# Keys, values and transposes of a full step moved between the score blocks of a second cross-attention layer

## The reference

```python
x = x + _L1_xattn_ref(_layernorm(x, axis=-1), ctx_1024, ctx_1024, wq, bq, wk, bk, wv, bv, wo, bo)

def _L1_xattn_ref(query, key, value, wq, bq, wk, bk, wv, bv, wo, bo):
    NUM_HEAD, DIM_HEAD = 16, 16
    Q = proj(query, wq, bq)        # x @ w.T + b, split into 16 heads of 16
    K = proj(key, wk, bk)
    V = proj(value, wv, bv)
    energy = einsum('bhqd,bhkd->bhqk', Q, K) / sqrt(DIM_HEAD)
    attn = softmax(energy, axis=-1)
    out = einsum('bhqk,bhkd->bhqd', attn, V)
    return out.transpose(0, 2, 1, 3).reshape(B, S, DIM) @ wo.T + bo
```

## Time and profile before

| | |
|---|---|
| median of 3 runs | 1888.92 us (1888.12 to 1889.22) |
| the profiled execution, its own time | 1879.97 us |
| its span | 1878.3 us, mean granted clock of PE 0.93 |
| busy, share of the span | PE 85%, PEld 64%, DVE 60%, ACT 42%, POOL 27% |
| `cross1`, t = 9 to 40 | 1151.6 to 1678.2 us, by the first exponential of each step |

### The profile page before, as it was taken

How to read it: one execution, slowest core, us unless ns; L and a number is a source line. 1 busy time by engine, 2 the same in 40 slices (tenths; PEclk the granted TensorE clock), 3 DMA queues, 4 the chain that set the end, 5 groups by cost and what they waited for, 6 DMA issues and landing times. The chain is left out here.

```text
span 1878.3 us, 26909 instructions
## 1 busy us (share of the span) xinstructions
PE 1603.4 (85%) x10311; PEld 1193.4 (64%) x10311; DVE 1122.9 (60%) x1784; ACT 790.6 (42%) x1084; POOL 500.8 (27%) x630
## 2 busy tenths in 40 slices
PE   5989999999999668779997787998999899875299
PEld 3777777777777457558887564555665555433288
DVE  3976666666652465356665798777666777005641
ACT  3545555555544132224442223555555555651110
POOL 0004434434469000000000202444333544640000
PEclk9999999999999877679999999999999899997599
DMA  2122212212222100022221110110010010000253
GB/s 79 57 57 68 66 48 68 65 49 68 57 57 46 34 1 1 22 92 81 77 95 38 34 46 23 35 35 24 23 35 23 25 33 12 1 1 23 90 170 110
DMA packets 75443, 92.35 MB, mean 49 GB/s; under 512 B 7442, under 2 KB 62276, under 8 KB 75332
## 3 DMA queue, kind: packets, MB, share of 16 engines
q1 hardware_dynamic: 75140, 90.79, 16.3%
q10 hardware_dynamic: 192, 0.05, 0.0%
HBM read 73.47 MB, written 0.52 MB: 39 GB/s over the span
## 5 line engine op out<-in xcount | busy, mean ns | idle before, releaser
L591 POOL CAST st<-ef 32x512 fp32r<-32x512 f32 x384 | 233.5, 608 | 369.2 <-PE score L1173 325.6
L1744 DVE TENSOR_REDUCE mx<-bank 128x1 f32<-128x512 f32 x384 | 246.9, 685 | 96.8 <-PE bank L1188 96.1
L777 ACT ACTIVATE P<-score 128x1024 f32<-128x1024 f32 x256 | 251.3, 1023 | 124.7 <-PE score L1173 124.6
L977 PE MATMUL bank<-c_hi,w_split 128*128 128x512 f32 x640 | 223.6, 407 | 26.1 <-DVE c_lo L1601 16.1
L1173 PE MATMUL score<-qs,st 97*128 97x512 f32 x512 | 174.1, 429 | 16.8 <-ACT P L777 11.5
L1188 PE MATMUL bank<-ef,qm 128*128 128x512 f32 x384 | 151.1, 445 | 30.1 <-DVE mx L1744 21.0
L977 PEld LDWEIGHTS bank<-c_hi,w_split 128*128 128x128 f32 x640 | 122.9, 192 | 73.6 <-issue 22.4
L556 POOL TENSOR_TENSOR sum<-sum,P 128x512 f32<-128x512 f32 x84 | 111.1, 1323 | 209.9 <-ACT P L693 209.9
L693 ACT ACTIVATE P<-score 128x1024 f32<-128x1024 f32 x128 | 130.0, 1025 | 78.5 <-PE score L1011 76.1
L977 PE MATMUL bank<-w_split,c_hi 128*128 128x256 f32 x768 | 145.7, 289 | 5.4 <-ACT v L787 5.4
L1188 PEld LDWEIGHTS bank<-ef,qm 128*128 128x128 f32 x384 | 73.1, 192 | 100.5 <-DVE mx L1744 80.5
(11 more groups left out here) (320 smaller groups left out, 2809.4 us busy)
## 6 DMA issues: line engine op xcount, KB each, us to landing
c_in<-in_ctx SPq DMA_DIRECT2D x64, 512.0 KB, 3.9
w<-k SPq DMA_DIRECT2D x128, 128.0 KB, 2.2
arena<-in_L_ffn_w SPq DMA_DIRECT2D x16, 1024.0 KB, 5.2
arena<-in_L_ffn_W SPq DMA_DIRECT2D x16, 1024.0 KB, 5.5
x<-in_x SPq DMA_DIRECT2D x1, 512.0 KB, 3.7
raw<-in_L_xattn_Wk SPq DMA_DIRECT2D x1, 512.0 KB, 6.5
raw<-in_L_xattn_Wv SPq DMA_DIRECT2D x1, 512.0 KB, 7.3
raw<-in_L_xattn_Wq SPq DMA_DIRECT2D x1, 512.0 KB, 8.2
```

The lines of the kernel that those rows point to most:

```text
L591: pool.tensor_copy(st1[32 * block:32 * block + 32, k, :], ef1[rows, g % LAG, part, :].bitcast(F32)).then_inc(a[f"st{k}"], 16)
L777: act.activation(P1[:, index % PRING, :], score[n % 2][:], ACT.Exp).then_inc(a["p"], 1)
L977: last = mm(dst, l, r, start=(n == 0), stop=(n == len(pairs) - 1))
L1744: v.tensor_reduce(mx1[:, u % 2, i, n:n + 1], bank_of(a, g + 1, f"m{n}")[:], AX.X, ALU.max).then_inc(a["red"], 1)
```

## The change

Three edits, all in `cross1`. The numbers of lines behind the change are up to 15 higher: L964 becomes L972, L977 L985, L1173 L1181, L1188 L1196, L1201 L1210, L1601 L1616, L1744 L1759, L1755 L1770.

1. A full step now transposes the next chunk, t + 1, and does so behind blocks 6 and 7. Keys stand behind block 1 and values behind blocks 3 and 5. The mixture's second half moves behind block 1 of the next step. All eight blocks have their two maxima behind them. In steps with i = 0 (t = 16, 24) keys, mixture, values, shift row and transposes stay behind block 7. From t = 33 on, each block has one mixture block behind it, four blocks late.
2. `order1` follows, and serves all steps.
3. The ring `ef1` of keys gets ten slots (`ERING`) in place of nine; other buffers move to make room.

```diff
+ERING = LAG + 1
-        ef1 = at("ef1", 0, [LAG, 2, CHUNK], F32R)
-        v1 = at("v1", 9216, [VRING, KT, 16, 17])
+        ef1 = at("ef1", 0, [ERING, 2, CHUNK], F32R)
+        v1 = at("v1", 10240, [VRING, KT, 16, 17])
...
-        wout1 = at("wout1", 31104, [4, D])
+        wout1 = at("wout1", 50176, [4, D])
...
-        order1 = ["t0", "t1", *(f"m{n}" for n in range(16)), "k0", "v0", "v1"]
-        early1 = ["k0", "v0", "v1", "t0", "t1"]
+        order1 = [*(f"m{n}" for n in range(16)), "k0", "v0", "v1", "t0", "t1"]
...
             if kind == "m":
-                return ("red", 16 * (t - 1) + n + 1) if t <= CHUNKS else None
-            chunk = t + (kind == "t" and t < LAG)
-            if not 0 <= chunk < CHUNKS or (kind == "t" and t < LAG <= chunk):
+                return ("red", 16 * (t - 1) + n + 1) if LAG <= t <= CHUNKS else None
+            chunk = t + (kind == "t")
+            if not 0 <= chunk < CHUNKS:
                 return None
...
@@ ScalarE, a full step
                     for n in range(8):
                         weights(g, n)
-                        if n in (1, 4) and t < CHUNKS:
-                            context_high(a, c_hi, t, t, n // 4)
...
+                        if i and t < CHUNKS:
+                            if n == 1:
+                                keys(t)
+                            if n in (3, 5) and u % 2 == 0:
+                                values(u, i, n // 2 - 1)
+                            if n >= 6 and t + 1 < CHUNKS:
+                                context_high(a, c_hi, t, t + 1, n - 6)
...
@@ TensorE, a full step
-                    ahead_of = 8 if i == 0 else 7 if u % 2 else 6
                     for n in range(8):
...
                         scores(g, n)
-                        if t <= CHUNKS and n < ahead_of:
+                        if t <= CHUNKS:
                             maxima(t - 1, n)
-                        if n in (1, 4) and t < CHUNKS:
-                            turn(a, t, t, n // 4)
-                        if n == 1 and t > CHUNKS + 1 and g % NCH:
-                            mixture(g - 1, 1)
-                        if n == 5:
-                            mixture(g, 0)
-                    if t < CHUNKS:
-                        keys(t)
-                    if t <= CHUNKS and ahead_of < 8:
-                        maxima(t - 1, ahead_of)
-                    if t <= CHUNKS or g % NCH == NCH - 1:
-                        mixture(g, 1)
-                    if t <= CHUNKS and ahead_of < 7:
-                        maxima(t - 1, 7)
-                    if t < CHUNKS and u % 2 == 0:
-                        values(t, 0)
-                    if i == 0 and t <= CHUNKS:
-                        shift_row(u - 1)
-                    if t < CHUNKS and u % 2 == 0:
-                        values(t, 1)
+                            if n == 1 and g % NCH:
+                                mixture(g - 1, range(4, 8))
+                            if n == 5:
+                                mixture(g, range(4))
+                        elif n >= 4:
+                            mixture(g, (n - 4,))
+                        elif t > CHUNKS + 1:
+                            mixture(g - 1, (n + 4,))
+                        if i and t < CHUNKS:
+                            if n == 1:
+                                keys(t)
+                            if n in (3, 5) and u % 2 == 0:
+                                values(t, n // 2 - 1)
+                            if n >= 6 and t + 1 < CHUNKS:
+                                turn(a, t, t + 1, n - 6)
+                    if i == 0:
+                        if t < CHUNKS:
+                            keys(t)
+                        mixture(g, range(4, 8))
+                        if t < CHUNKS and u % 2 == 0:
+                            values(t, 0)
+                        if t <= CHUNKS:
+                            shift_row(u - 1)
+                        if t < CHUNKS:
+                            if u % 2 == 0:
+                                values(t, 1)
+                            turn(a, t, t + 1, 0)
+                            turn(a, t, t + 1, 1)
...
@@ VectorE, a full step
-                    ahead_of = 8 if i == 0 else 7 if u % 2 else 6
                     for h in range(HPU1):
-                        if LAG <= t < CHUNKS and h == min(ahead_of + 1, 7):
-                            if ahead_of < 8:
-                                low_keys(t)
                         if LAG <= t <= CHUNKS:
                             reduce(t - 1, h)
...
-                        if t < LAG and h == 1:
+                        if (t < LAG and h == 1) or (i and LAG <= t < CHUNKS and h == 2):
                             low_keys(t)
-                        if LAG <= t < CHUNKS and h in (2, 5):
-                            context_low(a, c_hi, c_lo, t, t, h // 4)
                     if i == 0 and 0 < t <= CHUNKS:
                         maximum(u - 1)
-                    if LAG <= t < CHUNKS and ahead_of == 8:
+                    if i == 0 and LAG <= t < CHUNKS:
                         low_keys(t)
                     if g > 0 and g % NCH == 0:
                         finish(g // NCH - 1)
-                    if t + 1 < LAG:
+                    if t + 1 < CHUNKS:
                         for f in range(2):
                             context_low(a, c_hi, c_lo, t, t + 1, f)
```

More of the change, by code:

```diff
@@ L590, in stage_keys @@
                     for block, part in ((0, 0), (1, 0), (2, 1)):
[L591 removed]
+                        pool.tensor_copy(st1[32 * block:32 * block + 32, k, :], ef1[rows, g % ERING, part, :].bitcast(F32)).then_inc(a[f"st{k}"], 16)
                         pool.wait_ge(a[f"st{k}"], a.n(f"st{k}", 48 * g + 16 * block + 16))
@@ L819, in cross1 @@
                             values(u, i, 1)
-                        if t + 1 < LAG:
-                            for f in range(2):
-                                context_high(a, c_hi, t, t + 1, f)
+                        for f in range(2):
+                            context_high(a, c_hi, t, t + 1, f)
                         if t == NCH:
@@ L1187, in maxima, with mixture @@
                         dst = score[h % 2][:, 512 * q:512 * q + 512] if early else place_free(a, g + 1, f"m{2 * h + q}")[:]
-                        mm(dst, qm1[:, h, 128 * q:128 * q + 128], ef1[:, g % LAG, 0, :], start=True, stop=True).then_inc(a["ms"], 1)
-                def mixture(g, quad):
+                        mm(dst, qm1[:, h, 128 * q:128 * q + 128], ef1[:, g % ERING, 0, :], start=True, stop=True).then_inc(a["ms"], 1)
+                def mixture(g, blocks):
                     u, i = divmod(g, NCH)
-                    if i == 0 and quad == 0:
-                        clear_mix(a, u)
-                    if quad == 0:
-                        pe.wait_ge(a["v"], a.n("v", values1(u, i) + 2))
-                    for k in range(KT):
-                        index = 8 * g + 4 * quad + k
+                    for n in blocks:
+                        quad, k = divmod(n, 4)
+                        if n == 0:
+                            if i == 0:
+                                clear_mix(a, u)
+                            pe.wait_ge(a["v"], a.n("v", values1(u, i) + 2))
+                        index = 8 * g + n
                         pe.wait_ge(a["p"], a.n("p", index + 1))
```

41 lines of the change are left out of this document (16 added, 25 removed).

## The result

The changed kernel takes 1961.22 us (median of four runs, 1951.45 to 1965.97), the kernel before 1888.52 us in the same comparison. The ratio is 1.0383, with a 95% interval of 1.0336 to 1.0429: it is slower by 72.7 us. The forecast was 1951, range 1924 to 1978, slower with a chance of 0.93. The way, the place and most of the size were right. In the stage itself the sum had 62 us and the profiled execution shows 73; about half of the 11 us between them are shown to be the clock in ordinary steps (E6).

A forecast was written before the change was run, and what follows sets the result against it. PE and DVE handing two PSUM banks back and forth were taken as the bound. Stretch terms of +18.7, +13.0, +12.2, +8.7, +12.8, +1.6, -5.3 and +0.6 gave +62 us, a median of 1951, range 1924 to 1978.

The forecast's parts named there:

- the sum: Fourth stage, t = 8 to 40: gains and losses of all stretches added, together +62 us.
- The second transpose waits for a `c_lo` behind all reductions: Full steps: PE waits before transpose f=1 for DVE's subtraction of f=0, behind sixteen reductions; 1.7 us a step.
- the lower bound: Steps with transposes: if `c_lo` found a gap before the last two reductions, 1.3 us less loss each; +33 in all.
- An odd-unit step takes 19.0, with low queries 20.1: Steps without values: 19.0 us in place of 16.1; low queries ahead of the reductions add 1.06.
- The split of the loss: Odd-unit step: of +2.9 us, 1.7 is the wait before the second transpose, 1.2 uncovered maxima in blocks 3 to 5.
- PE's own work of 13.3 us: Odd-unit step before the change: matmuls, keys, mixture and transposes sum to 13.3 us of 16.1.
- the circle: Odd-unit step: schedule of PE, ACT and DVE from one `c_lo` of f=0 to the next, closing at 19.0 us.
- Steps t = 16 to 18 and the half clock after `finish`: Unit edge: 25.2, 27.2 and 22.9 us, plus 2.5 for half clock; 77.8 for 64.8.
- The clock stays up in ordinary steps: Full steps away from `finish`: short waits leave the granted clock at 1.00, so the sum adds nothing.
- rival A: Ordinary steps: the clock falls there too, 10 to 32 us more, 1961 to 1983; chance 0.11 beyond the forecast.
- Rival B: Full steps: DVE limits less than scheduled, half the loss hidden; +15 to +45, 1904 to 1934; chance 0.14.
- C: Even-unit steps: values between blocks cover the waits for reductions; faster, median about 1882; chance 0.04.

The follow-up runs named there:

- E6: Changed kernel with 24 matmuls of zeros before the second transpose and 12 before the maxima of block 1: 1953.71 us, ratio 1.0366.
- E1: Changed kernel with `c_lo` of f=0 moved on DVE ahead of the last two reductions: 1949.55 us, ratio 1.0339.
- E10: E1 with matmuls of zeros (24 or 8, none at i = 1) before the maxima of block 1: 1926.61 us, ratio 1.0214.
- E3: Kernel before with only the mixture of t = 33 to 40 placed as in the change: 1878.16 us, ratio 0.997.
- E8: Changed kernel with maxima over half of each bank, so shorter reductions: 1902.55 us, one run.
- E7: Kernel before with maxima over half of each bank, so shorter reductions: 1839.25 us, one run.
- E5: Changed kernel with steps of i = 0 (t = 16, 24) placed like all other full steps: 1963.87 us, ratio 1.043.
- E9: E3 with transposes of its own chunk behind blocks 0 and 2, keys, values and mixture pairs spread, and `c_lo` and `low_keys` moved: 1852.22 us, ratio 0.9832.
- E4: Changed kernel with transposes, keys, values and mixture pairs spread evenly over the blocks: 1864.44 us, ratio 0.989.

## Why the prediction was right, and where it fell short

- *The second transpose waits for a `c_lo` behind all reductions:* right. 43.2 us in 22 waits, 1.4 to 2.2 us in twenty of them (1.7 in the forecast), 6.5 behind `finish` (5.4 + 1.7). E1 moves only that instruction, E10 it with zeros, and both get 1.26 us back in t = 30 at full clock, the 1.3 of the lower bound; E10 has 18.7 less than E6 in t = 9 to 30.
- *An odd-unit step takes 19.0, with low queries 20.1:* 19.03 and 20.2. *An even one 21.8:* 21.77 (t = 23), 22.13 (t = 22).
- *The last seven steps 9.8:* 9.76, shown alone by E3.
- *The split of the loss:* too much for uncovered maxima, too little for the chain (E8). PE's own work of 13.3 us was too small as well (14.5 without any idle time in E7; the sum of 38 matmuls at 0.24 is 9.1, not 8.9), but the circle, which gave the 19.0, doesn't use it.
- *Steps t = 16 to 18 and the half clock after `finish`:* 77.5 for 77.8, and this is luck. By steps 25.2, 27.2 and 25.4 were forecast and 28.1, 25.8 and 23.5 came: the first was 2.9 too short, the others 3.3 too long together. In t = 24 to 26, 2.1 over, it is the same, +3.9, +0.8 and -2.5. The lower clock didn't come behind `finish` alone: the granted clock was 0.94, 0.89, 0.94 in t = 16, 17, 18 and 0.84, 0.77, 0.98 in t = 24, 25, 26.
- *The clock stays up in ordinary steps (rival A apart from it, chance 0.11):* this is the step that failed. It fell in some ordinary steps, at full price in few: t = 20 took 25.05 for 22.93, t = 10 22.03 for 20.41. Filling the waits gives 5.4 us in the ordinary steps of this execution, and 13.0 would have been to gain in E5's. The sum had nothing for it, and A (10 to 32 us, up to 1.7 in 19 steps) began too high: one execution lies between the two cases that I had kept apart, the other inside A. A step with a fallen clock can also lose more than 1.7 (t = 15 took 21.69 in E5 for 19.16). The clock goes with the spread: two runs of the changed kernel with a mean granted clock of 0.911 and 0.912 took 1965.97 and 1964.98 us, two with 0.919 took 1951.45 and 1957.46. In t = 31 to 33 the clock was 0.90, and 2.0 us are missing there, but it was 0.92 before too: what this part owes to the clock is not shown.
- *Rival B (half of the loss hidden) and C (the values' cover wins):* refuted by the step lengths. That covering waits can win is shown by E9, with another order.

Open in part: the 1.7 us that t = 30 keeps over the kernel before in E1 and E10. E1's trace says where they lie: PE is idle 1.0 us for reductions and `c_lo` there against 0.2 before, and six of its eight pairs of maxima take 0.73 to 1.10 us instead of 0.63, before three. That the lump of mixture and keys and the uncovered blocks 3 to 5 are the reason is read from the timeline; no run took the lump alone apart.

## What to carry to other kernels

When a piece is moved to a new place in one engine's order, follow its answer through every other engine's order: here a subtraction of 0.68 us became late only because it stood behind sixteen reductions. Two uses of one bank in a row need the whole round (write, copy, subtract) between them, so put as much other work there. Spread pieces so that each handed-over bank has some work behind it, and check for every kind of step that the work is really there: in E4 two blocks of each odd step had none behind them. And price a new wait twice: once for its length, once for the slower clock it can leave behind, which can also take back the gain when the wait is shortened.

## What the runs showed of the hardware

I had not expected that added matmuls of zeros shorten a stretch: t = 10 to 15 took 122.6 us without and 119.0 with 216 more matmul records, because the granted clock went from 0.93 to 1.00. Nor that a stop of 1.5 us can be enough for the lower clock, and need not be. At the edge to t = 20 the clock fell behind such a stop and before the next one, of 0.7 us: the pair of maxima at 1403.76 already takes 1.05 us, 0.63 at full clock.

```profile
1402.71 0.66 PE L972 MATMUL bank<-ident,c_in 128*128 128x128 f32 x4 [1.51 <-DVE c_lo L1616]
1403.12 0.84 PE L1181 MATMUL score<-qs,st 97*128 97x512 f32 x2
...
1403.76 1.05 PE L1196 MATMUL bank<-ef,qm 128*128 128x512 f32 x2
...
1406.40 1.39 PE L1196 MATMUL bank<-ef,qm 128*128 128x512 f32 x2 [0.73 <-DVE mx L1759]
...
1407.72 3.21 PE L1210 MATMUL bank<-P,v 128*17 128x256 f32 x32
```

The same two waits, 1.48 and 0.60 us, left t = 30 at full speed, and the same instructions kept the clock in t = 27 in the changed kernel's trace and lost it in E5's. The Trainium skill, "TensorE: Matmul & The Clock Gate", section "A second HAM failure mode: psum-queue depth-cycling", tells of such a swing between the two levels from short pauses between groups of matmuls; this case's traces agree in t = 10 to 25 (granted clock 0.85 to 0.93); in t = 27 to 30 the changed kernel's shows none (1.00) and E5's does (0.94).
